# One-hot rows of layer 1 turned back by TensorE instead of made by VectorE

## The chip, the cores and the metric

One Trainium2 chip, of which the kernel uses one core. The metric is the time of one execution on the device in microseconds (us), the median of several runs.

## The reference

Four graph layers run one after the other on 6250 nodes of 128 features and 100000 edges sorted by destination; behind each stands a residual and a layer norm. The change touches the first, a graph attention layer with self loops:

```python
h = x @ W
a_s = h @ att_src
a_d = h @ att_dst
e = leaky_relu(a_s[src] + a_d[dst], 0.2)
e = exp(e - segment_max(e, dst)[dst])
denom = segment_sum(e, dst)
out = segment_sum(h[src] * (e / (denom[dst] + 1e-16))[:, None], dst)
x = layernorm(x + out + bias)
```

Layer 2 weighs its messages by a filter of each edge, softplus(edge_attr_128 @ We1 + be1) @ We2 + be2. That filter depends on no node, so the kernel computes it during layer 1.

## The kernel before

Nodes lie in 49 blocks of 128 (NB). Edges, sorted by destination block, are cut into 832 steps (STEPS) of at most 128 edges, each of one block. Four steps (GRP) make a tick, so there are 208 ticks (TICKS). Edges stand on the partitions. For a step, GpSimd gathers the 128 source rows from gat_table (h, a one, a_s) by an indirect DMA (line 2354) into a ring of RT = 14 ticks. The one-hot matrix of a step says which edge belongs to which of the block's 128 nodes. It is needed in two positions: hot_t (nodes on the partitions, bf16, made from the row of local places, gat_turn, L842) and hot (edges on the partitions, f32, made by gat_hot, L929, a comparison of iota_free with local). ScalarE weighs hot in place by exp of the edge's logit (gat_weigh, L1603), and one matmul of a step, hot times the gathered rows (gat_product, L2026, two f32 passes), gives its sums, 129 columns wide. VectorE adds them to the block's running sum with a rescale (gat_sum, L946), because the maximum is a running one.

Each engine runs a loop over turns T (t in the code) of its own. A function with lag k works on tick T - k in turn T, and engines meet by semaphores alone. TensorE's turn is written in this order: a piece of the sort of a second list (background), every fourth turn gat_pair (L2016, 16 small matmuls that spread the running maxima), gat_product of T - 11, gat_mask of T - 2 (L2003, four transposes of the gathered a_s, and L2005), f_filter of T - 4 (L2035, L2036), f_hidden_of of T - 2 (L2044). VectorE's turn is woven round by round: gat_top of T - 3 (L849, the maximum over the mask's bank), every fourth turn a step of gat_max (L864 to L895) and of gat_logit (L905 to L922), the first sum of gat_sum of T - 12, gat_hot of T - 9, gat_turn of T - 1 (L842), after that round a piece of the sort (mostly L590 and L591; L571 and L575 at a flip; two pieces in every fifth turn), then the second sum, f_plus_of of T - 3 (L953), the third and the fourth sum. In a turn with T divisible by 4, VectorE also loads registers ahead of its first sum (L832). ScalarE's turn is f_made_of of T - 5 (L1625), f_soft of T - 3 (L1615, L1617, L1619), small operations every fourth turn (L1585, L1591 to L1596), gat_weigh of T - 10, and last its piece of the sort. f_hidden_of waits for the L953 of the tick before it, L953 for L1619, L1615 for f_hidden_of.

Some pieces of the sort are turned steps: TensorE transposes the keys in two halves (L1908), ScalarE copies each half from PSUM (L1512), and TensorE waits for the copies at the head of its turn.

The second list serves later layers and is in the same loop. PSUM has eight banks: 0 and 1 serve the filter, 2 the mask, 3 the sort, 4 and 5 (by the tick's parity) the sums of steps 1 to 3 of a tick, 6 and 7 the sum of step 0, and bank 6 also gat_pair's result. hot has three buffers, hot_t nine. Waits on them: gat_hot waits for the product three ticks back, the product for the sums two ticks back, and GpSimd's gather of tick t for product_done of tick t - 14.

A matrix ident_b, the identity in bf16, is written at L1308 in the stage behind layer 1.

## Time and profile before

| what | us |
|---|---|
| runs, median (lowest to highest of 3) | 3761.26 (3758.0 to 3769.63) |
| profiled execution, whole | 3758.77 |
| its span | 3756.9 |
| VectorE busy in the span | 2426.8 |
| TensorE busy in the span | 2837.3 |
| first and last gather of layer 1 start | 158.4, 1339.5 |
| first mask, last sum of layer 1 start | 191.4, 1370.6 |

All times in rows count from the start of the span. PE is TensorE's matmuls, PEld its weight loads, DVE is VectorE, ACT ScalarE, POOL GpSimd. In a row of a stretch the busy times follow in the order PE, PEld, DVE, ACT, POOL, each with its instructions in brackets; then come the clock granted to TensorE as a share of its full 2.4 GHz, the DMA engines' share and GB/s. A timeline's row gives start, duration, engine, line, operation, written and read tiles, and in square brackets how long the engine was idle ahead of it and who ended that. Neighbouring operations of one engine overlap by some 0.1 us, so what one costs in a full list is the distance from its start to the next one's, not its duration. Waits that have the word issue as their end are those that no semaphore explains.

### The profile page before, as it was taken

What the parts mean: (1) busy time and instruction counts of PE and PEld (TensorE: products, weight loads), DVE (VectorE), ACT (ScalarE), POOL (GpSimd) and SP (SyncE); (2) the same over time, 40 slices, a digit from 0 to 9 for tenths busy, and PEclk for the clock granted to TensorE, in tenths of its full rate; (3) what the DMA queues carried; (4) which work ended last, traced back from release to release, by engine and by line L of the source; (5) the groups of instructions that cost most, each with busy time, mean ns of one, the idle gap of its engine ahead of it and who ended that gap; (6) DMA issues with size and microseconds to landing.
All of it is one profiled execution on the core that took longest, in us unless ns stands there. A gap on an engine that the chain in (4) does not pass through costs nothing.

```text
span 3756.9 us, 64520 instructions
## 1 busy us (share of the span) xinstructions
PE 2837.3 (76%) x18791; PEld 2148.5 (57%) x18791; DVE 2426.8 (65%) x9159; ACT 1854.4 (49%) x4465; POOL 1848.2 (49%) x1971
## 2 busy tenths in 40 slices
PE   7477777777777857666566666666666899999998
PEld 7356656566665646666455555555554555566665
DVE  5489988889887988999666766666666322221111
ACT  3067666666666741000278888888888111111111
POOL 0377777667766743333677777777774000000000
PEclk9799999999998968988788888888887899999999
DMA  2776666666556618999444444444443555555553
GB/s 59 137 170 161 158 151 149 145 148 153 144 143 151 154 33 261 326 320 323 132 127 129 134 133 132 139 132 128 129 132 113 220 197 200 204 213 197 199 198 138
DMA packets 429661, 621.44 MB, mean 165 GB/s; under 512 B 64854, under 2 KB 329358, under 8 KB 416505
## 3 DMA queue, kind: packets, MB, share of 16 engines
q1 hardware_dynamic: 282927, 403.18, 34.0%
q0 software_dynamic: 75296, 179.75, 18.5%
q10 hardware_dynamic: 71082, 34.28, 3.2%
q8 instruction: 160, 2.62, 0.3%
q14 instruction: 196, 1.61, 0.1%
HBM read 414.86 MB, written 202.10 MB: 164 GB/s over the span
## 4 chain that ended last, share of the span: by engine, by line
PE 39%; DVE 32%; issue 12%; DMA 6%; ACT 5%; DVEq 3%; POOL 1%; ACTq 1%; SPq 0%; POOLq 0%
PE bank L2228 21%; DMA message_table<-arena 5%; DVE acc L946 4%; PE bank L2281 4%; DVE acc L1086 3%; PE bank L2258 3%; PE bank L2259 3%; DVE arena L1350 2%; DVE arena L591 2%; DVE arena L842 2%; PE bank L2319 2%; DVE arena L1149 2%; DVE local L1122 2%; DVE arena L590 2%; PE bank L2044 2%
## 5 line engine op out<-in xcount | busy, mean ns | idle before, releaser
L2354 POOL DMA_INDIRECT arena<-gat_table,pick x832 | 857.6, 1031 | 346.1 <-issue 244.1
L2354 POOL DMA_INDIRECT arena<-message_table,pick x832 | 815.8, 980 | 256.1 <-issue 249.2
L1755 ACT ACTIVATE arena<-arena 128x257 bf16<-128x257 f32 x1250 | 575.2, 518 | 5.2 <-DMA arena<-row_starts 5.2
L2281 PE MATMUL bank<-arena 128*128 128x128 f32 x1664 | 377.0, 325 | 194.1 <-issue 113.9
L1086 DVE TENSOR_TENSOR acc<-acc,bank 128x128 f32 x832 | 236.5, 284 | 335.7 <-PE bank L2281 305.2
L2281 PEld LDWEIGHTS bank<-arena 128*128 128x128 f32 x1664 | 303.3, 234 | 239.0 <-issue 135.9
L1239 DVE TENSOR_REDUCE arena<-bank 128x128 f32<-128x384 f32 x98 | 50.2, 552 | 580.8 <-PE bank L2228 580.8
L1745 ACT CAST arena<-bank 128x512 bf16<-128x512 f32 x625 | 363.9, 583 | 114.9 <-PE bank L2259 78.2
L2228 PE MATMUL bank<-arena 128*128 128x384 bf16 x2401 | 404.2, 327 | 8.0 <-DMA arena<-adjacency 8.0
L2228 PE MATMUL bank<-arena,acc 128*128 128x384 bf16 x2401 | 401.1, 325 | 0.0
L2124 PE MATMUL bank<-arena 128*128 x1664 | 261.7, 315 | 119.3 <-DVE arena L1350 90.3
L2228 PEld LDWEIGHTS bank<-arena 128*128 128x128 bf16 x2401 | 235.5, 98 | 164.1 <-issue 11.2
L2228 PEld LDWEIGHTS bank<-arena,acc 128*128 128x128 bf16 x2401 | 233.7, 97 | 154.8
L946 DVE SCALAR_TENSOR_TENSOR acc<-acc,arena,bank 128x129 f32 x832 | 285.7, 343 | 50.7 <-issue 22.6
L2124 PEld LDWEIGHTS bank<-arena 128*128 128x128 f32 x1664 | 234.6, 222 | 146.2 <-issue 145.5
L1762 ACT ACTIVATE rstd<-moments,eps_col 128x2 f32<-128x2 f32 (+1 forms) x50 | 14.8, 295 | 595.7 <-DVE moments L1249 595.7
L2036 PE MATMUL bank<-w_L_gnn_We,arena 128*128 128x128 f32 x1568 | 288.9, 307 | 0.0
L1615 ACT ACTIVATE arena<-bank,c_L_gnn_be 128x512 f32<-128x512 f32 x196 | 135.2, 690 | 303.2 <-PE bank L2044 300.6
L2026 PEld LDWEIGHTS bank<-arena 128*128 128x128 f32 x1664 | 237.3, 211 | 81.0 <-issue 65.6
L1603 ACT ACTIVATE arena<-arena 128x128 f32<-128x128 f32 x832 | 263.7, 389 | 22.4 <-DVE arena L929 22.3
L2258 PE MATMUL bank<-arena,pick 128*128 128x256 bf16 x624 | 189.5, 321 | 105.5 <-ACT arena L1745 61.3
L2036 PEld LDWEIGHTS bank<-w_L_gnn_We,arena 128*128 128x128 f32 x1568 | 243.3, 196 | 33.0 <-issue 3.8
(369 smaller groups left out, 5727.1 us busy)
## 6 DMA issues: line engine op xcount, KB each, us to landing
adjacency<-arena SPq DMA_DIRECT2D x125, 640.0 KB
message_table<-arena POOLq DMA_DIRECT2D x208, 256.0 KB, 5.4
filter_table<-arena SPq DMA_DIRECT2D x196, 256.0 KB
arena<-adjacency SPq DMA_DIRECT2D x25, 1600.0 KB
acc<-adjacency SPq DMA_DIRECT2D x25, 1600.0 KB
arena<-adjacency SPq DMA_DIRECT2D x25, 1536.0 KB
acc<-adjacency SPq DMA_DIRECT2D x25, 1536.0 KB
xt<-edge_cols SPq DMA_DIRECT2D x131, 256.0 KB
```

The source lines that it names most:

```text
L946: e.scalar_tensor_tensor(a, a, small["scale"][:, g % 2, q + s:q + s + 1], sum_place(t, s), ALU.mult, ALU.add).then_inc(summed, 1)
L1086: e.tensor_tensor(a, a, banks[t % len(banks)][:, s * P:(s + 1) * P], ALU.add).then_inc(sums, 1)
L1603: ins = e.activation(hot[t % 3][:, s, :], hot[t % 3][:, s, :], ACT.Copy, scale=weight[:, s:s + 1])
L1745: e.copy(staged[n // CHUNK % 2][:, 2 * (n % CHUNK):2 * (n % CHUNK) + 2, :], bank_of_pair(n)[:, :].rearrange("p (k d) -> p k d", k=2)).then ...
L1755: ins = e.activation(pair_sign[j % PAIR_RING][:, k, :], row_start[w % ROWS_DEEP][:, :], ACT.Sign, scale=-1.0, bias=edge_at[:, q:q + 1])
L2026: ins = e.matmul(sum_place(t, s), hot[t % 3][:, s, :], gathered[:, slot(t, s), 0:D + 1], start=True, stop=True)
L2036: ins = e.matmul(bank[1][:, s * P:(s + 1) * P], magn[u % 2][:, s * P:(s + 1) * P], mats["L1_gnn_We2"][:, :], start=False, stop=True)
L2124: ins = e.matmul(spread_bank(n)[:, s * P:(s + 1) * P], hot_n[n % HN][:, s * P:(s + 1) * P], xn[:, bass.ds(b, 1), :].rearrange("p o d -> p ...
L2228: ins = e.matmul(bank[2 * (w % 2) + k][:, 0:3 * D], units[u % UNIT_BUFS][:, at - UNIT_SB * h, k * P:(k + 1) * P], node_parts[layer][:, at, ...
L2258: e.matmul(to, pair_src[n % PAIR_RING][:, 0, k, :], signs[:, k, 0:WN], start=True, stop=False)
L2281: ins = e.matmul(banks[n % depth][:, s * P:(s + 1) * P], hots[n % depth][:, s, :], gathered[:, slot(n, s, DEPTH[layer]), 0:D], start=True, ...
L2354: e.indirect_dma_start(out=dst, out_offset=None, in_=table, in_offset=bass.IndirectOffsetOnAxis(ap=index, axis=0)).then_inc(done, 16)
```

## The change

gat_hot goes, and with it the semaphore hot_made. TensorE gets two functions. gat_back turns the four bf16 squares of hot_t of tick T - 9 by a transpose against ident_b, into bank 7 as bf16; it waits for hot_turned and, since the bank is single, for ScalarE's weighing of the tick before. gat_last makes the product of a tick's fourth step in bank 6, behind a wait for all sums of the tick before. Both stand at the end of TensorE's turn, behind f_hidden_of; gat_product keeps steps 0 to 2, in bank 4 or 5. product_done now counts with gat_last. ScalarE reads bank 7 instead of hot, writes hot, and waits for hot_back and for the product three ticks back. gat_turn waits for hot_back nine ticks back as well. gat_pair's result moves to bank 4, its wait on the sums by two steps. ident_b is written ahead of the loop.

```diff
--- before.py
+++ after.py
@@ -469,10 +469,10 @@
         l_in = [sem(f"places_in{k}") for k in range(2)]
         m_hot, m_spread, m_made = (sem("message_" + n) for n in ("hot", "spread", "made"))
         m_out = [sem(f"message_out{k}") for k in range(MT)]
-        (hot_turned, masked, max_taken, dst_put, parts_split, hot_made, paired, pair_taken,
+        (hot_turned, masked, max_taken, dst_put, parts_split, hot_back, paired, pair_taken,
          edge_made, weight_made, scale_made, hot_weighted, product_done, summed) = (
             sem("gat_" + n) for n in ("hot_turned", "masked", "max_taken", "dst_put", "parts_split",
-                                      "hot_made", "paired", "pair_taken", "edge_made", "weight_made",
+                                      "hot_back", "paired", "pair_taken", "edge_made", "weight_made",
                                       "scale_made", "hot_weighted", "product_done", "summed"))
         vec = sem("vector_own")
         degree_turned, degree_kept, degree_summed, degree_rooted = (
@@ -532,11 +532,12 @@
             return f_value(max(range(u % UNIT_BUFS, TICKS, FT))) + 16 * (u // UNIT_BUFS + 1)
 
         def sum_place(t, s):
-            if s == 0:
-                return bank[6 + t % 2][:, 0:D + 1]
-            return bank[4 + t % 2][:, (s - 1) * (D + 2):(s - 1) * (D + 2) + D + 1]
-
-        pair_place = bank[6][:, 2 * P:2 * P + 6 * GW]
+            if s == GRP - 1:
+                return bank[6][:, 0:D + 1]
+            return bank[4 + t % 2][:, s * (D + 2):s * (D + 2) + D + 1]
+
+        pair_place = bank[4][:, 3 * (D + 2):3 * (D + 2) + 6 * GW]
+        back_place = bank[7][:, 0:GRP * P // 2].bitcast(BF16)
 
         def steps_before(at):
 
@@ -839,6 +840,7 @@
                     e.wait_ge(local_row_in[t % 3], 16 * (t // 3 + 1))
                     if t >= HT:
                         e.wait_ge(paired, (t - HT) // GT + 1)
+                        e.wait_ge(hot_back, t - HT + 1)
                     e.tensor_scalar(hot_t[t % HT][:, :], local_row[t % 3][:, :], iota_part[:, 0:1], None, ALU.is_equal
                                     ).then_inc(hot_turned, 1)
                     yield
@@ -920,15 +922,6 @@
                     yield
                     after(q)
                     e.tensor_tensor(edge2, edge2, both[:, :, 1], ALU.subtract).then_inc(edge_made, 1)
-                    yield
-
-                def gat_hot(t):
-                    i = t * GRP
-                    if t > 2:
-                        e.wait_ge(product_done, t - 2)
-                    e.tensor_tensor(hot[t % 3][:, :, :], iota_free[:, :].unsqueeze(1).to_broadcast([P, GRP, P]),
-                                    local[0][:, i:i + GRP].unsqueeze(2).to_broadcast([P, GRP, P]),
-                                    ALU.is_equal).then_inc(hot_made, 1)
                     yield
 
                 def gat_sum(t):
@@ -1015,7 +1008,7 @@
                     for lag, fn in ((6, gat_max), (8, gat_logit)):
                         if (t - lag) % GT == 0 and 0 <= t - lag < TICKS:
                             pieces.append(fn((t - lag) // GT))
-                    for lag, fn in ((12, gat_sum), (9, gat_hot), (1, gat_turn)):
+                    for lag, fn in ((12, gat_sum), (1, gat_turn)):
                         if 0 <= t - lag < TICKS:
                             pieces.append(fn(t - lag))
                     if 0 <= t - 3 < FTICKS:
@@ -1305,7 +1298,6 @@
                         e.wait_ge(buckets_in, 16 * BG)
                         own(e.memset(far_rows[:, :], FAR_ROW))
                         own(e.tensor_copy(iota_b, iota_free[:, :]))
-                        own(e.tensor_copy(ident_b, ident[:, :]))
                         own(e.tensor_scalar(block_base[:, :], iota_free[:, 0:SBS], -float(PLACES), 0.5, ALU.mult, ALU.add))
                         q = own(e.tensor_scalar(bucket_part[:, :], bucket_keys[:, :], KEY_MASK, 7, ALU.bitwise_and,
                                                 ALU.logical_shift_right))
@@ -1457,6 +1449,7 @@
                                    in1=rows["L0_gnn_att_dst"][:, :], scale=1.0, scalar=0.0,
                                    op0=ALU.mult, op1=ALU.add, accum_out=gat_w[:, D + 1:D + 2]).then_inc(gat_w_made, 1)
             e.wait_ge(gat_w_made, 1)
+            own(e.tensor_copy(ident_b, ident[:, :]))
             own(e.tensor_scalar(below_diag[:, :], iota_free[:, :], iota_part[:, 0:1], None, ALU.is_gt))
             e.wait_ge(fold_done, 2)
             own(e.tensor_tensor(half_row[:, :], bank[4][:, P:2 * P], rows["L1_gnn_b3"][:, :], ALU.add))
@@ -1598,9 +1591,12 @@
                 def gat_weigh(t):
                     weight = small["weight"][:, t // GT % 2, t % GT * GRP:(t % GT + 1) * GRP]
                     e.wait_ge(weight_made, t // GT + 1)
-                    e.wait_ge(hot_made, t + 1)
+                    e.wait_ge(hot_back, t + 1)
+                    if t > 2:
+                        e.wait_ge(product_done, t - 2)
                     for s in range(GRP):
-                        ins = e.activation(hot[t % 3][:, s, :], hot[t % 3][:, s, :], ACT.Copy, scale=weight[:, s:s + 1])
+                        ins = e.activation(hot[t % 3][:, s, :], back_place[:, s * P:(s + 1) * P], ACT.Copy,
+                                           scale=weight[:, s:s + 1])
                     ins.then_inc(hot_weighted, 1)
 
                 def second_list():
@@ -2009,7 +2005,7 @@
                     if g:
                         e.wait_ge(pair_taken, g)
                     if g > 1:
-                        e.wait_ge(summed, (g * GT - 6) * GRP + 1)
+                        e.wait_ge(summed, (g * GT - 6) * GRP + 3)
                     for j in range(GW):
                         t, s, c = g * GT + j // GRP, j % GRP, (g * GW + j) % SPAN + 1
                         o = pair_place[:, 6 * j:6 * j + 6].rearrange("p (k a) -> p k a", a=2)
@@ -2022,10 +2018,24 @@
                         e.wait_ge(summed, (t - 1) * GRP)
                     if t % GT == 2:
                         e.wait_ge(pair_taken, min(t // GT + 2, TICKS // GT))
+                    for s in range(GRP - 1):
+                        e.matmul(sum_place(t, s), hot[t % 3][:, s, :], gathered[:, slot(t, s), 0:D + 1],
+                                 start=True, stop=True)
+
+                def gat_last(t):
+                    if t:
+                        e.wait_ge(summed, t * GRP)
+                    s = GRP - 1
+                    e.matmul(sum_place(t, s), hot[t % 3][:, s, :], gathered[:, slot(t, s), 0:D + 1],
+                             start=True, stop=True).then_inc(product_done, 1)
+
+                def gat_back(t):
+                    e.wait_ge(hot_turned, t + 1)
+                    if t:
+                        e.wait_ge(hot_weighted, t)
                     for s in range(GRP):
-                        ins = e.matmul(sum_place(t, s), hot[t % 3][:, s, :], gathered[:, slot(t, s), 0:D + 1],
-                                       start=True, stop=True)
-                    ins.then_inc(product_done, 1)
+                        ins = e.transpose(back_place[:, s * P:(s + 1) * P], hot_t[t % HT][:, s * P:(s + 1) * P], ident_b)
+                    ins.then_inc(hot_back, 1)
 
                 def f_filter(u):
                     e.wait_ge(f_plus, u + 1)
@@ -2063,7 +2073,8 @@
                     weave([], background, background_turns(t))
                     if (t - 7) % GT == 0 and 0 <= t - 7 < TICKS:
                         gat_pair((t - 7) // GT)
-                    for lag, fn in ((11, gat_product), (2, gat_mask), (4, f_filter), (2, f_hidden_of)):
+                    for lag, fn in ((11, gat_product), (2, gat_mask), (4, f_filter), (2, f_hidden_of), (9, gat_back),
+                                    (11, gat_last)):
                         if 0 <= t - lag < (FTICKS if fn in (f_filter, f_hidden_of) else TICKS):
                             fn(t - lag)
                 for g in background:

```

## Rows read from the trace of the kernel before

**Rows 1.** Stretches: us, busy us (instructions) by engine, PEclk, DMA share, GB/s.

```profile
192.00:540.00 348.00, 272.50 (x1963) 210.16 (x1962) 328.17 (x833) 238.40 (x557) 270.90 (x254) 0.98 0.67 160
540.00:1197.00 657.00, 500.33 (x3548) 397.24 (x3548) 570.07 (x1505) 432.86 (x1026) 459.02 (x449) 0.94 0.61 146
```

**Rows 2.** The view of line 2354, GpSimd's gathers: durations, idle before, landing.

```profile
L2354 POOL DMA_INDIRECT arena<-gat_table,pick x832: 938/946/2299, 158.4 to 1339.5; - x167
...
  PE bank L2026: 70.5, 29
...
DMA to landing us min/median/max: 3.2/3.3/3.8
```

**Rows 3.** Timeline of GpSimd: start, us, engine, line, operation, idle before it.

```profile
480.91 0.95 POOL L2354 DMA_INDIRECT arena<-gat_table,pick  x1 [0.30 <-issue]
...
562.21 0.94 POOL L2354 DMA_INDIRECT arena<-gat_table,pick  x1 [0.76 <-PE bank L2026]
...
1197.57 0.94 POOL L2354 DMA_INDIRECT arena<-gat_table,pick  x1 [0.64 <-PE bank L2026]
```

**Rows 4.** Timeline of TensorE at the mask of tick 58.

```profile
492.88 0.60 PE L2003 MATMUL bank<-ident,arena 128*128 128x128 f32 x4
```

**Rows 5.** Timeline of VectorE in ordinary ticks and behind a turned one.

```profile
884.10 0.75 DVE L953 SCALAR_TENSOR_TENSOR arena<-bank,neg_L_gnn_be,arena 128x512 f32<-128x512 f32 x1 [0.83 <-ACT arena L1619]
...
887.04 0.34 DVE L946 SCALAR_TENSOR_TENSOR acc<-acc,arena,bank 128x129 f32 x1
887.29 0.69 DVE L929 TENSOR_TENSOR arena<-iota_free,local 128x512 f32<-128x512 f32 x1
887.89 0.48 DVE L842 TENSOR_SCALAR arena<-arena,iota_part 128x512 bf16<-128x512 uint8 x1
...
889.75 0.75 DVE L953 SCALAR_TENSOR_TENSOR arena<-bank,neg_L_gnn_be,arena 128x512 f32<-128x512 f32 x1
...
892.50 0.35 DVE L946 SCALAR_TENSOR_TENSOR acc<-acc,arena,bank 128x129 f32 x1 [0.48 <-issue]
...
895.33 0.74 DVE L953 SCALAR_TENSOR_TENSOR arena<-bank,neg_L_gnn_be,arena 128x512 f32<-128x512 f32 x1
...
897.43 0.34 DVE L946 SCALAR_TENSOR_TENSOR acc<-acc,arena,bank 128x129 f32 x1
...
900.18 0.74 DVE L953 SCALAR_TENSOR_TENSOR arena<-bank,neg_L_gnn_be,arena 128x512 f32<-128x512 f32 x1
...
902.54 0.35 DVE L946 SCALAR_TENSOR_TENSOR acc<-acc,arena,bank 128x129 f32 x1
...
909.86 0.34 DVE L946 SCALAR_TENSOR_TENSOR acc<-acc,arena,bank 128x129 f32 x1
```

**Rows 6.** Timeline of TensorE in the same stretch.

```profile
896.22 1.10 PE L2044 MATMUL bank<-xt,w_L_gnn_We 128*128 128x512 f32 x2 [1.60 <-DVE arena L953]
...
897.15 1.06 PE L2026 MATMUL bank<-arena 128*128 128x129 f32 x8
898.05 0.60 PE L2003 MATMUL bank<-ident,arena 128*128 128x128 f32 x4
898.48 0.38 PE L2005 MATMUL bank<-arena,far 128*128 128x512 bf16 x1
...
905.90 0.66 PE L1908 MATMUL bank<-ident,arena 128*128 128x128 f32 x4 [3.31 <-ACT arena L1512]
906.39 1.06 PE L2026 MATMUL bank<-arena 128*128 128x129 f32 x8
...
909.27 1.02 PE L2044 MATMUL bank<-arena,w_L_gnn_We 128*128 128x512 f32 x2
```

**Rows 7.** The views of lines 1908, 1625 and 1617: min/median/max ns.

```profile
L1908 PE MATMUL bank<-ident,arena x112: 271/273/477, 546.8 to 1106.1; 128*128 128x128 f32 x112
L1625 ACT COPY arena<-bank x196: 560/567/589, 202.3 to 1302.2; 128x512 f32<-128x512 f32 x196
L1617 ACT ACTIVATE arena<-arena x209: 417/632/636, 195.2 to 2904.3; 128x512 f32<-128x512 f32 x104, 128x256 f32<-128x256 f32 x1
```

## The prediction

> **What bounds the kernel now.** I read the stretches by engine first. Layer 1's edge loop runs from 192 to 1371 us, and VectorE is the busiest engine: 328 of 348 us up to 540, 570 of 657 us up to 1197 [rows 1]. A share is no bound, so the waits come next. GpSimd, which gathers four times per tick, waited 70.5 us in 29 times for a product of TensorE, because its ring of 14 ticks was full [rows 2]. The first such wait ends at 562.21, the last but three at 1197.57, and those three are of 0.3 us [rows 3]. From 1197.57 it gathers without a stop to 1339.5 [rows 2], and the stage ends 31 us later. So the stage's end is set by the last release that GpSimd waited for. Until then the consumers (VectorE, TensorE, ScalarE) set it, and a gain of theirs counts only by what it takes off these 70.5 us. Before 540 they may gain only as far as rows lie ready: for tick 58 the last gather starts at 480.91 and lands 3.3 us later, its mask starts at 492.88, 8.7 us of slack [rows 2 to 4].
>
> In an ordinary tick VectorE's list is closed: one operation follows the other [rows 5]. TensorE meanwhile waits for L953, 1.60 us in one tick [rows 6]. Hence VectorE bounds ordinary ticks, at 4.85 to 5.65 us each.
>
> **What goes.** L929, once per tick, starts at 887.29 and its follower at 887.89: 0.60 us of VectorE's list [rows 5]. If nothing else came, 208 x 0.60 = 125 us, of which GpSimd's waits let 70.5 count.
>
> **What comes.** Four bf16 transposes per tick. The nearest row is L2003, four transposes from 898.05, with the next matmul at 898.48: 0.11 us each, so 0.44 [rows 6]. Bounds: nothing, if they fall into TensorE's waits; and four times the 0.273 that one transpose of L1908 lasts, 1.1, if they don't overlap [rows 7]. I take 0.44, since kind and width are the same. The Trainium skill (TensorE: Matmul & The Clock Gate, Part 4: PE-mode transpose) gives some 275 ns for a 128x128 bf16 transpose inside a kernel, and says that transposes do not count as activity for the clock. By that figure the block would take 1.1 us and the sum would be rival C's. The rows speak against it as a pitch: 0.273 is a duration here too [rows 7], but four overlap [rows 6].
>
> ScalarE's L1603 now reads PSUM, four times a tick. The 512-wide copy from PSUM takes 0.567, a 512-wide operation from SBUF 0.632 [rows 7]; bounds 0 and -0.065 us each; I take -0.05, 0.2 per tick, which counts only where ScalarE is on the path. The bf16 identity, one 128x128 copy, moves ahead of the loop, beside work that waits for the histogram; I cost it at nothing, and at no more than the 0.34 of an operation of that width [rows 5] if uncovered.
>
> **The new loop.** TensorE's order in a turn becomes three products, mask, filter, hidden (L2044), transposes, fourth product. VectorE's first sum of the next turn waits for that fourth product, and hidden waits for L953, which follows this sum on VectorE. Before, the product stood a whole turn ahead of its sum. Queued behind the waiting first sum are L842, the sorting pair L590/L591, the second sum and L953; TensorE's hidden and all behind it wait for L953. The part off VectorE: end of L953 (896.07) to hidden 0.15; hidden to the next matmul 0.93 [rows 5, 6]; transposes 0.44; two of the eight passes that take 1.06 are 0.24 and 0.16 more till the last is out; 0.05 to VectorE. Together 1.97 us from the end of L953 to the first sum.
>
> Now each kind of ordinary tick, by VectorE's rows (plus is slower). From L953 at 884.10 (end 884.85): allowed from 886.82, it ran at 887.04, so the whole 0.60 is gained. From 889.75 (end 890.50): allowed 892.47, and L905 (0.24) with the register load of 0.48 now stand behind the same wait, so the sum starts at 893.19 where it ran at 892.50: 0.69 late, less the 0.60, +0.09. From 895.33 (end 896.07): allowed 898.04 against 897.43: +0.01. From 900.18 (end 900.92): 902.89 against 902.54: -0.25 [rows 5]. Every fifth tick has a second sorting pair behind L953, which covers the wait: -0.60. Over twenty ticks, 5 x 0.60 + 4 x 0.15 + 3 x 0.60 = 5.4, or 0.27 us per tick, not 0.60.
>
> **Ticks with a turned sort step.** L1908's 112 transposes, eight a step, make 14 [rows 7]; six more ticks over 9 us come from the table behind the sort. In one, TensorE waits 3.31 us, to 905.90, for ScalarE's copy, queued behind L1603 [rows 6]. Here a quarter of the product block (0.22) leaves the path and ScalarE gives 0.2. But in the next tick hidden stands at 909.27, so the first sum can't start before 909.27 + 0.93 + 0.44 + 0.40 + 0.05 = 911.09, where it ran at 909.86: +1.2 - 0.6 = +0.6 [rows 5, 6]. Per event about +0.2; unfavourably +1.0.
>
> **A later release.** The ring's slot is free with the fourth product. Where the block ended at 907.45, that is 911.04: 3.6 us later for every wait of GpSimd [rows 6].
>
> **Sum**, till the last wait of GpSimd: ticks 8 to 66, 59 x 0.27 = 16, capped by the slack of 8.7 at tick 58 plus the ticks after it, 11 gained. Ticks 67 to 170, 104 less three for each of 14 turned steps, 62 x 0.27 = 17 gained. Twenty events, 4 lost. Some ten ticks without a sorting pair, where TensorE is full, 10 x 0.3 = 3 lost. Release, 3.6 lost. Net gain 17.4, say 18 with the identity off the second stage's list. GpSimd's waits go from 70.5 to about 53. The tail of 31 us after the last gather holds ten turns, 3.1 each, VectorE's sums and L929 between. Afterwards L929 is gone, but the last sum's bank is single: four sums of 0.34 [rows 5] and 0.44 + 0.40 + 0.05 for TensorE make 2.3 at least, more at a lower clock. I take nothing, 3 us either way.
>
> The profiled execution took 3758.8 us, of which the span is 3756.9; 3758.8 - 18 = 3741. The median of the runs is 3761.3, 2.5 above: forecast 3743 us.
>
> **Rivals.** B, gather-bound: the part off VectorE is shorter than 1.97 (the transposes fall into waits), all 0.6 per tick is gained, GpSimd never waits. For it: from L953's end to the first sum VectorE had 1.3 to 2.2 us of work anyway [rows 5]. Against: the register load behind the wait. It gives 3761.3 - 70.5 + 3 = 3694 us. In a sentence that the sum does without: the Trainium skill (GPSIMD Engine Reference, Key points) says that GpSimd contends with VectorE's operations of two SBUF inputs, and L929 is one; gathers last 938 ns at least [rows 2], and part of what they last beyond that would go too, but only in this rival would it count.
>
> C, the loop loses: transposes do not overlap (1.1 us), the part off VectorE is 2.63. Then the four kinds of tick stand at -0.16, +0.75, +0.67 and +0.41, in the mean +0.2 per ordinary tick with every fifth at -0.6; 121 x 0.2 = 24, events 20 x 1.0 = 20, release 4: slower by 48, 3809 us. Between 0.11 (18 faster) and 0.27 (48 slower) it changes sign near 0.15 us per transpose. For it: one L2003's duration. Against: the pitch of four [rows 6].
>
> D, the gain is eaten: events cost 1.0 instead of 0.2 (16 more), so the change is worth -2 us: 3759 us. For it: post-event ticks have TensorE full. That the change doesn't do what it says I leave at next to nothing: L929 has no other issuer in this loop.
>
> **Numbers.** Forecast (3725 to 3756) 0.50, B 0.12, C 0.16, D 0.22. About 0.3%, 11 us, can be told from no change, so faster means below 3750: 0.8 x 0.50 + 0.12 = 0.52. Same: 0.10 + 0.18 of D = 0.28. Slower, C and the far side of D: 0.20. The range runs from B's 3692 to 3770, which leaves C and bits out.
>
> **What would show it.** Of after: VectorE waits at its first sum (and at L905's successor) for TensorE's fourth product in most ordinary ticks, 0.3 to 0.7 us; GpSimd's waits for it total some 50 us, none before 540, the last near 1180; four transposes per tick at a pitch of 0.11; ordinary ticks 0.27 shorter. Wrong would be GpSimd waits near zero (B), a pitch of 0.27 (C), or post-event ticks over 1 us longer (D). Gathers awaited by masks before 540 are expected and mean the cap was reached.

## The result, and the profile after

The changed kernel takes 3804.54 us, the median of 5 runs (3790.07 to 3809.97), against 3761.42 for the kernel before: ratio 1.01, interval 1.0084 to 1.0115. It is slower by some 43 us, where the prediction had it 18 us faster. The execution profiled after took 3790.07 us, of which its span is 3788.2, the fastest of the five; that of before spans 3756.9.

The stretches come first, by the same two windows as [rows 1]; the columns are those of [rows 1].

```profile
192.00:540.00 348.00, 284.61 (x2104) 223.85 (x2135) 288.77 (x756) 228.72 (x545) 260.05 (x250) 0.95 0.66 157
540.00:1197.00 657.00, 519.69 (x3857) 418.25 (x3908) 496.46 (x1354) 416.45 (x1007) 448.15 (x436) 0.93 0.62 144
```

VectorE's busy time fell: 288.8 us where it had 328.17, and 496.5 where it had 570.07 [rows 1]. The busy time that was to go did go, and yet the stage is longer, so the waits must have grown. TensorE's granted clock fell too, to 0.95 from 0.98 in the first stretch. GpSimd's view of its gathers, and three of them in its timeline (start, us, engine, line, operation, idle before):

```profile
L2365 POOL DMA_INDIRECT arena<-gat_table,pick x832: 938/945/2057, 158.0 to 1368.1; - x167
...
  PE bank L2029: 116.7, 61
```

```profile
233.65 0.94 POOL L2365 DMA_INDIRECT arena<-gat_table,pick  x1 [0.86 <-PE bank L2029]
```

```profile
1223.78 0.94 POOL L2365 DMA_INDIRECT arena<-gat_table,pick  x1 [0.47 <-PE bank L2029]
...
1368.14 0.94 POOL L2365 DMA_INDIRECT arena<-gat_table,pick  x1 [0.30 <-issue]
```

GpSimd waits for a product 116.7 us in 61 times, not 70.5 in 29 [rows 2], the first time at 233.65 instead of 562.21 and the last over 0.3 us at 1223.78 instead of 1197.57 [rows 3]. Its last gather starts at 1368.1, 28.6 us later than 1339.5 [rows 2]: all but 3 us of the 31 between the two spans. (The medians are 43 apart; the rows can account for the 31 of the two profiled executions.)

Who made the products late? VectorE's waits in us, times and longest, of the changed kernel (L939 is the sum, L907 the reduction of the logit), and of the kernel before (there L946):

```profile
DVE acc L939 <- PE bank L2029: 81.8, 101, 3.1
DVE acc L939 <- issue: 75.4, 53, 2.0
...
DVE arena L907 <- PE bank L2029: 31.9, 43, 2.7
...
DVE acc L939 <- DVE acc L939: 20.0, 129, 0.5
```

```profile
DVE acc L946 <- issue: 22.6, 43, 1.2
...
DVE acc L946 <- DVE acc L946: 19.7, 127, 0.2
...
DVE acc L946 <- PE bank L2026: 1.8, 3, 0.8
```

Ahead of sums and reduction VectorE waits 81.8 + 75.4 + 31.9 + 20.0 = 209 us, where it waited 22.6 + 19.7 + 1.8 = 44. That is 165 us of new waiting, for some 125 us of work saved (208 times 0.60). 114 of it carries the name of the fourth product (L2029), as forecast in kind; but 53 us more is "issue", at 53 sums instead of 43, which I had taken as unchanged. One such turn, VectorE's timeline:

```profile
886.63 0.74 DVE L946 SCALAR_TENSOR_TENSOR arena<-bank,neg_L_gnn_be,arena 128x512 f32<-128x512 f32 x1
...
888.04 0.69 DVE L851 TENSOR_REDUCE arena<-bank 128x4 f32<-128x512 f32 x1
889.22 0.26 DVE L907 TENSOR_REDUCE arena<-bank 128x32 f32<-128x96 f32 x1 [0.49 <-PE bank L2029]
891.12 0.35 DVE L939 SCALAR_TENSOR_TENSOR acc<-acc,arena,bank 128x129 f32 x1 [1.65 <-issue]
```

TensorE's beside it:

```profile
887.51 1.10 PE L2054 MATMUL bank<-xt,w_L_gnn_We 128*128 128x512 f32 x2
888.45 0.39 PE L2037 MATMUL bank<-r_L_gnn_att_src,arena 128*128 128x128 bf16 x4
888.67 0.44 PE L2029 MATMUL bank<-arena 128*128 128x129 f32 x2
888.95 0.83 PE L2022 MATMUL bank<-arena 128*128 128x129 f32 x6
```

And the chain of waits through it (start, us, what):

```profile
888.83 0.29 PE bank L2029 x2
...
889.22 0.26 DVE arena L907
889.47 1.31 DVEq L833
```

L946 ends at 887.37, the fourth product at 889.11, and L907 runs at 889.22: 1.85 us off VectorE, close to the 1.97 of the forecast. But L907 ends at 889.48 and the sum starts at 891.12, 1.65 us later, and 1.31 of them are VectorE's register load L833, queued between the two. The view of that load, in this turn of the changed kernel and in the turn of before whose sum is at 892.50 [rows 5]:

```profile
L833 DVEq TENSOR_LOAD <-blk_ints x1: 1548/1548/1548, 889.2 to 889.2; - x1
```

```profile
L832 DVEq TENSOR_LOAD <-blk_ints x1: 1103/1103/1103, 891.1 to 891.1; - x1
```

Before, the load began at 891.1 and took 1.10 us, while VectorE was still busy with L849 and L905; only its end stuck out, the 0.48 us of [rows 5]. After, it begins at 889.2, when L907's wait ends, and takes 1.55 us with one reduction of 0.26 to cover it. So it goes through the layer. The views of all 52 loads of the edge loop, after and before:

```profile
L833 DVEq TENSOR_LOAD <-blk_ints x52: 1095/1498/1642, 233.5 to 1390.3; - x52
```

```profile
L832 DVEq TENSOR_LOAD <-blk_ints x52: 1095/1100/1134, 231.3 to 1361.0; - x52
```

In 46 of the 52 turns of after, the load starts within 0.06 us of L907's start; before, it starts 0.70 us ahead of L905 in the median. A load that starts when the wait ends is also longer itself, 1.50 us in the median where it was 1.10; why, no run shows. By this turn the miss is 52 x (1.65 - 0.48) = 61 us, by the two lists of waits 53.

### The profile page after: what moved, and what is told of

Same layout as the page of the kernel before. It is cut to its first block, busy times and chain, and to the rows that moved or that the text cites. A ratio compares the mean times of both kernels' runs of the same rounds, so it can differ in the third digit from the quotient of the medians.

```text
span 3788.2 us, 66082 instructions
## 1 busy us (share of the span) xinstructions
PE 2894.9 (76%) x19522; PEld 2203.6 (58%) x19623; DVE 2312.4 (61%) x8951; ACT 1837.9 (49%) x4465; POOL 1844.9 (49%) x1971
## 4 chain that ended last, share of the span: by engine, by line
PE 45%; DVE 25%; issue 11%; DMA 6%; ACT 5%; POOL 3%; DVEq 3%; ACTq 1%; SPq 1%; POOLq 0%
PE bank L2239 21%; DMA message_table<-arena 5%; PE bank L2054 4%; PE bank L2292 4%; POOL arena L2365 3%; PE bank L2269 3%; PE bank L2270 3%; DVE acc L1079 3%; DVE arena L591 2%; DVE acc L939 2%; DVE arena L592 2%; DVE arena L946 2%; PE bank L2330 2%; DVE arena L1342 2%; DVEq L833 2%
## 5 line engine op out<-in xcount | busy, mean ns | idle before, releaser
L2365 POOL DMA_INDIRECT arena<-gat_table,pick x832 | 850.9, 1023 | 382.8 <-issue 234.7
L2292 PEld LDWEIGHTS bank<-arena 128*128 128x128 f32 x1664 | 307.1, 237 | 230.9 <-issue 158.0
L939 DVE SCALAR_TENSOR_TENSOR acc<-acc,arena,bank 128x129 f32 x832 | 286.3, 344 | 181.9 <-PE bank L2029 81.8
L2135 PEld LDWEIGHTS bank<-arena 128*128 128x128 f32 x1664 | 227.1, 215 | 152.0 <-issue 151.5
L2269 PE MATMUL bank<-arena,local 128*128 128x256 bf16 x626 | 190.6, 321 | 95.8 <-ACT arena L1741 57.8
L1598 ACT ACTIVATE arena<-bank,arena 128x128 f32<-128x128 bf16 x832 | 235.3, 365 | 28.4 <-issue 20.3
```

Source lines behind the costliest of these rows:

```text
L939: e.scalar_tensor_tensor(a, a, small["scale"][:, g % 2, q + s:q + s + 1], sum_place(t, s), ALU.mult, ALU.add).then_inc(summed, 1)
L1598: ins = e.activation(hot[t % 3][:, s, :], back_place[:, s * P:(s + 1) * P], ACT.Copy, scale=weight[:, s:s + 1])
L2135: ins = e.matmul(spread_bank(n)[:, s * P:(s + 1) * P], hot_n[n % HN][:, s * P:(s + 1) * P], xn[:, bass.ds(b, 1), :].rearrange("p o d -> p ...
L2269: e.matmul(to, pair_src[n % PAIR_RING][:, 0, k, :], signs[:, k, 0:WN], start=True, stop=False)
L2292: ins = e.matmul(banks[n % depth][:, s * P:(s + 1) * P], hots[n % depth][:, s, :], gathered[:, slot(n, s, DEPTH[layer]), 0:D], start=True, ...
L2365: e.indirect_dma_start(out=dst, out_offset=None, in_=table, in_offset=bass.IndirectOffsetOnAxis(ap=index, axis=0)).then_inc(done, 16)
```

## The experiments

Each expectation stands as it was recorded. The theory that formed from these rows: the load's latency, exposed behind a wait that the change put ahead of it, is the miss. The expectations of x1 to x12 call it R, those of x14 call it L; in those of x1, x2 and x4, L is the rival that only the late fourth product costs. The other rivals are the transposes and losses in the turned steps.

**The load moved ahead (x1, and again x14).** The load is issued in the turn before, ahead of L907's wait:

```
+                    if g > 1:
+                        block_registers(0, (g - 1) * GT)
...
-                    block_registers(0, t)
+                    if t == 0 or t == TICKS - GT:
+                        block_registers(0, t)
```

> The changed kernel with one edit: in every fourth turn VectorE loads its block registers ahead of L907's wait (in gat_logit) instead of behind it (in gat_sum). Theory R (register load): in the changed kernel the load of 1.1 to 1.2 us starts only once L907 has waited for the fourth product, and leaves VectorE idle 1.65 us where 0.48 was left before; ahead of the wait it hides. VectorE's idle time of kind issue ahead of the first sum falls from 75 us to under 25, and the kernel from 3804 to about 3750 us, 50 to 60 less. Theory L (only the wait for the fourth product costs, wherever the load stands): the idle time turns into a longer wait for the product, and the kernel stays within 10 us of 3804.

Measured: 3713.35 us, ratio to the kernel before 0.9859 (0.9843 to 0.9876). One moved load turns the sign of the change: 91 us under the first measurement of the changed kernel, though not on the same chip, and more than the 50 to 60 of the expectation. So the two were timed side by side:

> The changed kernel unaltered, as the base of the other three of this call. Every theory: slower than the kernel before by 0.5 to 1.2%, some 40 us on a chip where the kernel before takes 3765.

> Only the place of the register load differs from the changed kernel: it is issued in the turn before, ahead of the wait for the fourth product. Theory L (the load's latency behind the wait, 1.17 us in some 52 turns, is all of the miss): 60 us less than the changed kernel, ratio to it 0.984. Theory K (the load's delay also comes back through GpSimd's ring, which is filled later, so that it counts more than once): 80 to 95 us less, ratio 0.976 to 0.979.

Measured: changed 3798.26 (ratio 1.0103, 1.008 to 1.0127), load ahead 3717.43 (0.9882, 0.9865 to 0.9898). The load's place is worth 81 us, inside K's band and beyond the 60 of theory L. That K's way, through GpSimd's ring, is what makes the difference isn't shown. VectorE's timeline and waits of x14 (L947 is the sum, L910 the reduction), GpSimd's below, and the waits of x13:

```profile
888.16 0.26 DVE L910 TENSOR_REDUCE arena<-bank 128x32 f32<-128x96 f32 x1 [0.43 <-PE bank L2037]
888.46 0.35 DVE L947 SCALAR_TENSOR_TENSOR acc<-acc,arena,bank 128x129 f32 x1
```

```profile
DVE acc L947 <- PE bank L2037: 69.4, 103, 3.2
...
DVE arena L910 <- PE bank L2037: 32.4, 41, 3.0
...
DVE acc L947 <- issue: 2.4, 4, 1.6
```

```profile
POOL arena L2373 <- PE bank L2037: 37.0, 22, 4.6
```

```profile
DVE acc L939 <- PE bank L2029: 95.0, 101, 2.6
DVE acc L939 <- issue: 77.1, 52, 2.0
```

The sum now follows the reduction at once (888.16 + 0.26, then 888.46). "Issue" went from 77.1 to 2.4 us, which is 75 of the 81; the wait for the product went from 95.0 to 69.4, another 26; L851, for its own inputs, gave 10 back. The second term is a knock-on. Of the first, some 20 us aren't the change's doing: in the turns with a load, VectorE stood idle ahead of the first sum for 78 us in x13, 4.6 in x14 and 24 in the kernel before. Some of the knock-on may be the clock: over the loop, TensorE was busy 35 us longer in x13 for the same instructions, at a lower granted clock (x13, then x14).

```profile
192.00:1380.00 1188.00, 952.82 (x7009) 762.78 (x7109) 905.26 (x2472) 744.36 (x1817) 834.83 (x813) 0.92 0.62 145
```

```profile
192.00:1300.00 1108.00, 917.92 (x7012) 735.42 (x7111) 906.12 (x2474) 743.64 (x1817) 828.26 (x813) 0.96 0.66 156
```

How the 26 us divide between the clock and a fill of GpSimd's ring that comes later, no run separates.

**The late product without transposes (x2).** The changed kernel with the one-hot rows made by VectorE again and no transposes, but the fourth product still behind hidden:

```
-                    for lag, fn in ((12, gat_sum), (1, gat_turn)):
+                    for lag, fn in ((12, gat_sum), (9, gat_hot), (1, gat_turn)):
...
-                    for lag, fn in (... (2, f_hidden_of), (9, gat_back),
+                    for lag, fn in (... (2, f_hidden_of),
```

> The changed kernel without its transposes: VectorE makes the one-hot rows again (0.60 us per tick) and ScalarE weighs them in SBUF, but the fourth product stays at the end of TensorE's turn, behind the wait for the sums, and VectorE's first sum waits for it. It isolates the late product. Theory L and R together (a loop of VectorE's first half of a turn, hidden and the fourth product): per tick 0.60 us more in VectorE's part, 0.22 less in TensorE's, so some 0.38 x 190 = 70 us slower than the changed kernel, about 3870 us, 110 over the kernel before. If VectorE's list alone bounded (the loop immaterial): as the kernel before, 3761 us, give or take 10.

Measured: 3852.64 us, 1.0228 (1.0211 to 1.0245), with 168 us of GpSimd's waits. The later fourth product, with the register load behind its wait as in the changed kernel, costs 87 us by itself, and the transposes are not needed for the loss. It is some 20 us less than expected.

**VectorE's operation alone (x3).** The kernel before without L929 after the third tick. The one-hot rows then aren't made anew: ScalarE weighs what stands in the buffer, behind a wait for the product three ticks back, and the sums come out other than the reference's. The rest of the computation is kept:

```
-                        if 0 <= t - lag < TICKS:
+                        if 0 <= t - lag < (3 if fn is gat_hot else TICKS):
```

> The kernel before without VectorE's one-hot rows of edges from the fourth tick on; ScalarE weighs whatever stands in the buffer, so the sums are not the reference's. No transposes, no late product. It is the worth of taking L929 away by itself. If gathers bound behind it: GpSimd's waits for a product fall from 70.5 us to near 0, and the kernel from 3761 to 3690, no further. If the gain of a shorter list is lost to other waits (the filter's loop, turned steps): waits of 30 us or more remain and the kernel stands at 3720 or above.

Measured: 3692.38 us, 0.9797 (0.9781 to 0.9813). The groups of GpSimd's gathers (busy us, mean ns, idle us ahead), before and in x3:

```profile
L2354 POOL DMA_INDIRECT arena<-gat_table,pick x832 | 857.6, 1031 | 346.1 <-issue 244.1 <-PE bank L2026 70.5 <-DMA gat_table<-acc 30.7
```

```profile
L2355 POOL DMA_INDIRECT arena<-gat_table,pick x832 | 839.4, 1009 | 304.9 <-issue 248.4 <-DMA gat_table<-acc 30.4 <-PE bank L2027 24.6
```

The time is the expected one, and rival B's 3694 too, but not for B's reason alone. GpSimd's waits for a product fell by 46 us, to 24.6 and not to near 0. Another 18 us came from the gathers themselves, which the prediction had taken as fixed. The last wait over 0.4 us ends at 1133.59, and from there the gathers run on without a long stop and set the end.

**Only the fourth sum waits for the fourth product (x4).** The load stays where it was; the product's semaphore counts twice a tick. L907's wait, ScalarE's and GpSimd's are put in the new count as well, L907's behind three products, the other two behind the fourth:

```
-                    e.wait_ge(product_done, t + 1)
+                    e.wait_ge(product_done, 2 * t + 1)
...
+                        if s == GRP - 1:
+                            e.wait_ge(product_done, 2 * t + 2)
...
+                        ins = e.matmul(sum_place(t, s), ...)
+                    ins.then_inc(product_done, 1)
```

> The changed kernel with one edit: the first three sums of a tick, and L907, wait for the first three products only; just the fourth sum, which stands behind L946 on VectorE, waits for the fourth product. Theory L and R: the loop is cut, L907 waits no more, the load hides as before, GpSimd's waits fall below 20 us, and the kernel comes to 3690 to 3710 us, 50 to 70 faster than the kernel before. Rival T (TensorE's added work and the later release of the ring cost): the changed kernel's 3804 stays within 15 us, or falls no lower than 3761.

Measured: 3690.33 us, 0.9804 (0.9787 to 0.982), with 20.1 us of GpSimd's waits. It beats both kernels, the one before by 76 us. The waits of its sum (L941; L2032 is the fourth product):

```profile
DVE acc L941 <- PE bank L2032: 15.2, 28, 1.1
DVE acc L941 <- issue: 9.9, 19, 0.7
```

Two names share one thing here. By the timeline, all 15.2 us of the first line and 8.8 of the second lie ahead of the first sum of a turn with a load: 24.0 us, as before the change (24.0 too, in the same turns). L907 waits for nothing, the load takes its 1.10 us again, and it costs what it did. So the load is not dear by itself: it is dear behind a reduction that waited for the late product. The loss has one cause with two parts, a wait that was wider than the data it guards, and a load queued behind it.

**Both edits together (x16).** Its edit is that of x14 and that of x4.

> As x14, and the product semaphore counts twice per tick, so that the first three sums and the logit's reduction wait only for the first three products and the fourth sum for the fourth. If load and late product are two separate costs, both gone give less than either alone: some 3 to 10 us below the 3690 that the split alone gave beside a kernel before of 3766, ratio 0.977 to 0.980 to the kernel before. If they are one cost (the load hurts only because the late product ends the wait), this equals the split alone, 0.980 to 0.982, as the gathers are then the bound at some 3690.

Measured: 3684.99 us, 0.9796 (0.978 to 0.9813), 113 us below the changed kernel beside it and the fastest of all, though its interval doesn't part it from x4. It doesn't decide between the two theories either: the one gave 0.977 to 0.980, the other 0.980 to 0.982. VectorE's waits (L949 the sum, L910 the reduction, L844 the comparison of the turned rows) and GpSimd's view:

```profile
DVE arena L844 <- PE bank L2048: 39.8, 28, 3.5
...
DVE arena L910 <- issue: 12.1, 39, 0.8
...
DVE acc L949 <- PE bank L2040: 1.9, 3, 1.1
```

```profile
L2376 POOL DMA_INDIRECT arena<-gat_table,pick x832 | 840.4, 1010 | 297.6 <-issue 239.6 <-DMA gat_table<-acc 31.1 <-PE bank L2040 18.6
```

Waits for products ahead of sums are gone, but for 1.9 us. VectorE now runs ahead of TensorE and waits at L844 instead, 39.8 us. What that costs is not shown; GpSimd still waits 24.7 us for products of TensorE (18.6 for the fourth, 6.1 for the first three, whose line is not shown), so no more than that is left to gain from the consumers in this loop.

**The transposes twice over (x15, x14 as base).**

```
-                    for s in range(GRP):
+                    for s in (*range(GRP), *range(GRP)):
```

> As x14, but the four transposes that bring the one-hot rows back are made twice over in every tick, so TensorE makes eight. The second four write the same values again. If a transpose is worth 0.055 us in VectorE's loop, as the records of the changed kernel have it, four more add 0.22 us in some 110 ordinary ticks that count: 24 us more than x14, less where they fall into waits. At the 0.11 us of the prediction it is 48 us, at 0.27 us it is 120.

Measured: 3731.86 us, 0.9926 (0.991 to 0.9943), 14.4 us over x14. TensorE's timeline of x15:

```profile
885.42 0.61 PE L2045 MATMUL bank<-r_L_gnn_att_src,arena 128*128 128x128 bf16 x8
885.87 0.44 PE L2037 MATMUL bank<-arena 128*128 128x129 f32 x2
```

Eight transposes take 0.45 us from the first to the product behind them, 0.056 each, half of the 0.11 in the sum. Part of that doesn't count: 14.4 us came of it, where 0.22 in every tick would be 46. GpSimd's waits rose from 37.0 to 75.0 us, but its gathers took 13.9 us less (a mean of 1003 ns for 1020).

**On two other chips.** x5 to x8 ran on one, x9 to x12 on another chip; on both, every kernel is 12% slower (the kernel before takes 4211 and 4216 us). So these go by ratios to the kernel before beside them.

The load moved ahead in the kernel before, where L905 waits for nothing late:

> The kernel before with the load ahead of L905. Of the 0.48 us that the load leaves idle there in 43 turns (22.6 us over all) some goes, but the load of 1.1 us still has only L849's 0.6 us over it. Theory: same to 15 us faster, 3750 to 3765; and in no case the 91 us that the same edit gave in the changed kernel, which would mean that the load was as dear before the change.

Measured: 0.9971 (0.9949 to 0.9994). The same edit that gave 2.1% in the changed kernel is worth 0.3% here. The chips differ, but x12 below gives a floor on such a chip: the load ahead, even with eight transposes, is 1.3% faster than the changed kernel beside it (x9). It is the pair of load and wait that costs.

The register load was to be made twice in its old place, as x5 and again as x10, with the changed kernel beside it as x9. The edit is one more `block_registers(0, t)` behind the first:

> The changed kernel with the register load of every fourth turn made twice, at its old place behind L907's wait. Theory R: the second load costs its full 1.1 us in each of 52 turns, so 50 to 60 us slower than the changed kernel, some 3855 to 3865. If a load's latency is only an artefact of the record and not on the path: within 10 us of 3804.

> The changed kernel itself, once more, on the chip of the three that follow, to have its time beside theirs: the chip of the last four runs is some 12% slower for every kernel and holds none of it. Every theory: 1.0% slower than the kernel before, as in its first measurement.

> The changed kernel with the register load made twice behind L907's wait, beside the changed kernel on the same chip. Theory R: 52 x 1.1 = 57 us slower than the changed kernel at most, 40 to 60 expected. If the load's latency is not on the path: within 10 us of it.

Measured: x5 1.0044 (1.0024 to 1.0065); x9 1.0056 (1.0035 to 1.0076), x10 1.0057 (1.004 to 1.0074). The times are those of the changed kernel, and the traces say why. The views of the load in x9 and in x10, over the whole execution:

```profile
L833 DVEq TENSOR_LOAD <-blk_ints x104: 1095/1101/2510, 255.2 to 3353.5; - x104
```

```profile
L833 DVEq TENSOR_LOAD <-blk_ints x104: 1095/1102/2196, 259.7 to 3344.6; - x104
```

Both hold 104 loads, 52 of them in the edge loop, where x10 should hold 156; so does x5. As far as the traces show, the second load never ran. These two runs are more timings of the changed kernel, and what a second load costs stays open; the expectations of x5 and x10 are not tested. x9 misses its own expectation: the change costs 0.6% on this chip, not 1.0.

Only the logit's reduction released early (x6, and again x11): it waits for three products, all sums still for the fourth. Of the edit, the line of L907; all sums wait for `2 * t + 2`:

```
-                        e.wait_ge(product_done, g * GT - 3)
+                        e.wait_ge(product_done, 2 * (g * GT - 4) + 1)
```

> The changed kernel where L907 alone waits for the first three products; all four sums still wait for the fourth product, and the load stands behind L907 as it did. The load's place in the code is the changed kernel's, only what stands ahead of it no longer waits. Theory R: the load then runs under L851 and under the wait for the fourth product, and the kernel lands where the load ahead put it, 3705 to 3725. If it were L907's own wait or the load's place by itself, less than half of the 91 us comes back: 3760 or more.

> The changed kernel where L907 alone waits for three products, all sums for the fourth; the load's place in the code is as in the changed kernel. Theory R: it comes 80 to 95 us below the changed kernel, where the load ahead put it (ratio to the kernel before 0.985 to 0.990). If the load matters only by its place in the code: less than half of that.

Measured: x6 0.9889 (0.9851 to 0.9927), x11 0.9927 (0.9902 to 0.9953), against 1.0056 for the changed kernel: 60 us of 4241 or 1.4% by x11 and x9, less than the 2.1% of x14. The load then takes 1.10 us again and starts 0.70 us ahead of L907 (medians of x11): it runs beside the wait for the product instead of behind it, and that part comes back without moving the load at all. What stays is the wait of the sums.

Last, eight transposes with the load ahead (x8, again x12):

> The changed kernel with the load ahead (3713 us), where TensorE makes its four transposes twice. It prices TensorE's part of the loop. In the trace of after four of them take 0.22 us from first to the next matmul, so the loop gets 0.22 us longer: at 0.055 each, with the waits for the fourth product in some 70% of the ticks, 0.22 x 145 = 30 us in VectorE's list; what of it counts is at most that, 15 to 30 us, 3728 to 3743. If transposes cost 0.27 each (my rival C): over 100 us slower. If the loop is immaterial: within 5 us.

> The load ahead, and the four transposes made twice. Beside the load ahead alone (ratio 0.986 to the kernel before): 15 to 30 us more, ratio 0.990 to 0.994, if four transposes take 0.22 us of the loop; over 100 us more (ratio above 1.012) by my rival C's 0.27 each; under 5 us (0.986 to 0.987) if TensorE's part is covered.

Measured: 0.9933 (0.9888 to 0.9978) and 0.9931 (0.9906 to 0.9956). With no run of the load-ahead kernel beside them on those chips, they don't price the transposes; x15 does. Both lie within the recorded 0.990 to 0.994 and far below rival C's 1.012.

## Why the prediction was wrong, step by step

- **What bounds.** Right in kind: VectorE's list set the pace until GpSimd's last wait, and with 0.6 us per tick off it (x3) the kernel ends at 3692 us. That rival B had 3694 is in part luck: 24.6 us of waits stayed that it had at none, and 18 us came from shorter gathers that it had not.
- **What goes.** Right: VectorE's busy time in the two stretches fell by 39 and 74 us [rows 1].
- **The register load: the step that failed.** It read "L905 (0.24) with the register load of 0.48 now stand behind the same wait", and gave +0.09 us for that kind of tick. The 0.48 was not the load's price. It was what stuck out of a load of 1.10 us that began beside earlier work. Behind a wait nothing covers it: 1.65 us. The term is 1.17 us short in 52 turns, 61 us, which is what the forecast missed by; that the two agree so well is in part chance, as terms beside it were off as well. Moving the load ahead takes 81 us off (x13 against x14), but that takes away its old 0.48 as well. The row that would have told was within reach: the view of the load's own line, with its start and its 1.10 us. I read the idle time behind it only.
- **The new loop.** Right in kind and nearly in size: 1.85 us off VectorE, forecast 1.97. The waits for the fourth product are the first in the list of after. By parts, hidden comes 0.14 us behind L946's end, the transposes 0.94 behind that; they take 0.22 and not 0.44, the product 0.44, and 0.11 pass till L907.
- **Transposes.** 0.056 us each, taken at 0.11; a doubling costs 14.4 us (x15). The 0.11 came from L2003, said to be of the same kind and width, but its rows are f32 and those of the change bf16. Rival C's 0.27 us is not found: its loss was of the right size (3809 us) for a wrong reason. The Trainium skill (TensorE: Matmul & The Clock Gate, Part 4: PE-mode transpose) gives some 275 ns for each; here one lasts 219 ns and the next one starts 56 ns later, so the figure doesn't hold as a price inside a block of four.

```profile
L2037 PE MATMUL bank<-r_L_gnn_att_src,arena x832: 216/219/314, 223.7 to 1392.9; 128*128 128x128 bf16 x167
```

- **ScalarE from PSUM.** Taken at 0.05 us less than from SBUF, each. The two views, after and before:

```profile
L1598 ACT ACTIVATE arena<-bank,arena x832: 348/366/387, 225.8 to 1394.1; 128x128 f32<-128x128 bf16 x167
```

```profile
L1603 ACT ACTIVATE arena<-arena x832: 386/388/404, 226.1 to 1364.4; 128x128 f32<-128x128 f32 x167
```

  366 ns for 388: 0.022 us saved, less than half of the term. What that moved was not measured apart.
- **Turned steps.** The forecast had about +0.2 us each and said TensorE would be late next. In the changed kernel one such tick shows something that the forecast did not have. TensorE's timeline of it, and its windows around it (the granted clock stands behind the busy times):

```profile
899.34 0.78 PE L1904 MATMUL bank<-ident,arena 128*128 128x128 f32 x4 [3.14 <-ACT arena L1505]
899.91 1.50 PE L2022 MATMUL bank<-arena 128*128 128x129 f32 x6
...
905.50 0.83 PE L2022 MATMUL bank<-arena 128*128 128x129 f32 x6
```

```profile
895.60:899.34 3.74, 0.60 (x7) 0.36 (x5) 2.35 (x6) 3.59 (x11) 2.83 (x4) 1.00 0.76 196
899.34:902.40 3.06, 2.93 (x14) 2.81 (x16) 1.29 (x2) 0.59 (x1) 1.66 (x2) 0.56 0.44 84
```

  After a wait of 3.14 us the clock granted is 0.56, near the lower of its two levels (1.2 of 2.4 GHz), and three products (x6) take 1.50 us, where the next turn's take 0.83. Before, after 3.31 us of waiting, eight passes took 1.06 [rows 6], at a granted clock of 1.00 from 905.90 to 908.50. The forecast had no term for the clock. What all these ticks cost together was not measured apart.
- **GpSimd's waits.** Forecast some 50 us, none before 540, the last near 1180. They are 116.7, from 233.65, to 1223.78. With the load ahead they are 37.0 (x14), less than forecast, so their sum was off by the load. That there would be none before 540 was wrong by itself: 16.6 us of after lie there, and 5.1 of x14, the first at 235.25.
- **The sum.** With the load ahead the kernel takes 3717 us (x14), 26 us under the forecast of 3743. That is not yet the kernel of the forecast, which kept the load's old 0.48; an estimate from the 24 us of idle time before and the 4.6 of x14 is that this is worth up to 20 of the 26. The transposes, 0.22 us per tick too dear in the sum, are worth some 14 by x15. So the other terms were about right together, and no run prices them one by one.
- **The cap.** The prediction says of the consumers that "a gain of theirs counts only by what it takes off these 70.5 us". That did not hold. x4 gained 76 us with 50 us of waits gone. Its last gather starts 71.5 us earlier (1268.0 for 1339.5), and 16 of these come from shorter gathers (841.5 us busy for 857.6). x15 waits 75.0 us, more than the kernel before, and is 31 us faster. The waits tell where the consumers set the pace, but the gathers' own time differs by as much as 31 us between kernels (834.6 in x15, 865.4 in x2), and shorter gathers only turn into more waiting while the consumers bound.
- **The gathers.** In a sentence apart: the Trainium skill (GPSIMD Engine Reference, Key points) has GpSimd contend with VectorE's operations of two SBUF inputs. The trace agrees in direction: taking L929 alone away (x3) brought the mean from 1031 to 1009 ns, 18 us in 832 gathers, against 5 us between two profiles of the changed kernel (1023 and 1029 ns). But x14 and x15, both without L929, differ by 14 us, so how much is L929's doing isn't settled.

## What to carry to other kernels

The idle time behind a latency-bound instruction in a trace is not its price but what happened to stick out of it; before a wait is put ahead of such an instruction, read its own start and duration and ask what will cover it then. Count in the trace of an experiment the instruction that its edit adds: in x5 and x10 it wasn't there. Move register loads ahead of the waits in their engine's queue, not behind them. When one of several products comes late, let only its own reader wait for it: one more count on a semaphore turned a change that lost 1% into one that gains 2% (x4, 76 us below the kernel before).

## What the runs showed of the hardware

A register load on VectorE's queue took 1.10 us in the edge loop of the kernel before, where it ran beside VectorE's work, and 1.50 in the median of the changed kernel, where it began with the end of a wait ahead of it. Four bf16 transposes of 128x128 follow each other at 0.056 us, four f32 ones at 0.11, while one of them lasts 0.219 and 0.273. TensorE's granted clock over the loop was 0.92 where it waited 158 us for VectorE ahead of hidden (x13) and 0.96 where it waited 99 (x14). After idle times of 3.14 and 3.31 us it was 0.56 in the changed kernel and 1.00 in the kernel before.
